# A pre-norm transformer block with routed experts on one core: block counts of the tensor-engine tiles read a turn ahead, gelus awaited singly, and the first batch's stacks moved through two DMA queues

## The chip, the core and the metric

The kernel runs on one core of one Trainium2 chip. Its engines are PE (TensorE, the matrix engine), ACT (ScalarE), DVE (VectorE), POOL (GpSimd) and SP (SyncE, which here only issues DMA transfers). The metric is the device time of one execution in microseconds (us); the kernel before has a median of 927.51 us over 3 runs (927.06 to 932.16).

## What is computed

The input x is 8 batches of 512 rows of 128 floats. Two blocks follow, each added to x:

```python
x = x + attn(layernorm(x))      # RMS norm; q, k, v; 16 heads of 8; then
#   lin: causal linear attention on Taylor features of q @ Wqf and k @ Wkf (order 2)
#   win: softmax attention, each query sees itself and 64 keys before it
#   attn(h) = h + concat(lin, win) @ Wout
x = x + ffn(layernorm(x))       # 8 experts, the two best of each row weighted
#   experts 0..3 (kind 0, "plain"): gelu(h @ W1 + b1) @ W2 + b2
#   experts 4..7 (kind 1, "kan"): basis functions of the layer norm of h, times kan_W0, a
#                                 second layer norm, basis functions again, times kan_W1
```

Which rows go to which expert depends on the data, so the number of tiles of each kind is known only on the chip.

## The kernel before, in words

All five engines have an instruction stream of their own, and semaphores order them. There are three stages.

**The prologue** (the streams up to `batches()`) prepares weights and the front of batch 0. DVE copies a mask pattern from PSUM (`band`, line 1027, once PE has raised `band_mm`), spreads it over two of three "stacks" of batch 0 (line 1030) and clears the PSUM tile `pv` (line 1036). PE transposes the normed rows (line 1425) and forms q, k and u (line 1428, SPLIT = q, k, u; u is the key side seen through the feature weights). Each is split into a half-precision part and a remainder: ACT writes `hi` (line 867), DVE writes `lo` (line 1042). SP stores `hi` and `lo` to the scratch `hl_d` in HBM (line 473: six stores of 128 KB, each pair awaiting its `lo`) and loads them back, rearranged by head, into the rows of the stacks (lines 448 and 450: 256 KB and 128 KB, one pair for each of the three stacks, semaphore `stack_loaded[0]`). SP then waits for all of them, and only then loads the rows `xb` of batch 1 (line 480). ACT clears a stack of batch 1 (line 875) after its part of the front; DVE spreads the pattern over the other two (line 1030 again).

**The batches.** `ORDER` lists the steps of a batch by hand; every engine walks the same list, `PROGRAM`, and does its part of each step. L, M and W are products on PE (lines 1588, 1569, 1601), each into one of three PSUM slots that ACT (lines 927, 936) or DVE (line 1185) frees; P is line 1629. Words with a plus are the front of the next batch: `stats` and `aggr` (DVE lines 994, 1003), `coef` (POOL lines 672 to 682 and the normed rows at line 691), `hT` (PE line 1425). POOL also masks diagonal blocks after an L step (line 766), and it scatters the routing records by indirect DMA (line 810). The step `out` is PE line 1688. The last batch is interleaved with the first tiles of the experts (`TAIL`, steps `ehid`, `efirst`, ...).

**The tiles.** A tile is 512 routed rows of one expert, four blocks of 128; a table in SBUF (`tab_i`, `tab_first`) gives for each tile its place, its expert and its number of filled blocks. A loop of UNROLL = 12 turns handles in turn k: for plain tiles `mlp_first(u+1)` in two parts (line 1475), `mlp_second(u+1)` (line 1493); for kan tiles `hidden_transposed(u)` (line 1530), `kan_first(u+1)` (line 1509), `rows_transposed` (line 1450) and `kan_second(u)` (line 1542). PE reads the number of blocks with `load_blocks`, a load from SBUF into a register of PE's sequencer, inside each of `mlp_first` (so twice a turn), `mlp_second`, `kan_first` and `kan_second`. In `mlp_first` it stands behind four waits:

```python
pe.wait_ge(m_y, tile_no(k, back=1))
if parts[-1] > 1:
    pe.wait_ge(m_g, tile_no(k, F // P, parts[-1] - 1))
...
with pe.If(load_blocks(0, k) > 2):
```

`m_g` counts the gelus of a tile (ACT line 885); the second part, `range(2, 4)`, writes the two PSUM banks that the first two gelus read. With more than two blocks both halves of 256 columns are multiplied, else one. DVE does the basis functions (line 1118), the statistics and the norm of the hidden rows (lines 1124 to 1141), and the weighting (lines 1103, 1107). POOL, in each turn, gathers kan rows (line 735), computes four norm coefficients (`hidden_coefficients`, line 760), scatter-adds the plain result (line 745), gathers plain rows, awaits that scatter, scatter-adds the kan result and awaits that (`end_of_add`).

## Time and profile before

| what | value |
|---|---|
| median of 3 runs | 927.51 us |
| the profiled execution | 928.66 us, of which its span in the trace is 926.8 us |
| PE, PE weight load | 765.3 us (83%), 571.6 us (62%) |
| ACT, POOL, DVE | 533.1 us (58%), 491.9 us (53%), 465.0 us (50%) |
| mean granted TensorE clock | 0.925 of full speed |

All moments below are microseconds from the start of the span: the prologue lasts to about 32, the batches to about 507, the tiles from there to the end. An engine's time is busy time; the time between is given with what ended it. "issue" is idle time for which the trace shows no semaphore: the sequencer was reading a register, branching or fetching.

### The profile page before, as it was taken

The page shows a single profiled execution, that of the slowest core. Times are in us where ns is not written, and L with a number is a line of the kernel's source. Part 1 is how long each engine was busy: PE and PEld are TensorE (multiplying, and loading weights), DVE is VectorE, ACT ScalarE, POOL GpSimd, SP SyncE. Part 2 cuts the span into 40 slices and gives each one's busy share as a digit, 9 for nine tenths or more (in the row PEclk, how much of TensorE's full clock was granted, in tenths as well). Part 3 has the DMA queues.
Part 4 walks back from the last instruction along what each step waited for, and adds up shares of the span by engine and source line. Part 5 has one row for each costly group of instructions (what it writes and reads, how often), then busy time and mean ns, then how long its engine had stood idle before and what let it go on. Part 6 is the DMA issues. An engine that isn't in the chain of part 4 may idle for free.

```text
span 926.8 us, 20634 instructions
## 1 busy us (share of the span) xinstructions
PE 765.3 (83%) x7113; PEld 571.6 (62%) x7114; DVE 465.0 (50%) x1076; ACT 533.1 (58%) x697; POOL 491.9 (53%) x699
## 2 busy tenths in 40 slices
PE   4599979799798797988945857999999999999870
PEld 2246555465454554546513645888988898889770
DVE  6525516355163362643501664565867785787330
ACT  4477756567475575666714626366677666766410
POOL 8334536545265254651572347548677767764431
PEclk9799989989899898999966979899999999999975
DMA  2330402204013040030162316255456446443213
GB/s 60 114 99 2 123 12 64 71 2 125 10 46 88 2 122 13 34 101 2 42 100 50 131 15 165 47 138 132 72 150 155 112 94 147 131 73 61 22 17 106
DMA packets 93698, 70.72 MB, mean 76 GB/s; under 512 B 41602, under 2 KB 85922, under 8 KB 91684
## 3 DMA queue, kind: packets, MB, share of 16 engines
q1 hardware_dynamic: 76660, 57.74, 22.0%
q0 software_dynamic: 16912, 11.35, 8.9%
q8 instruction: 72, 1.18, 0.6%
q14 instruction: 54, 0.44, 0.2%
HBM read 49.51 MB, written 21.36 MB: 76 GB/s over the span
## 4 chain that ended last, share of the span: by engine, by line
PE 59%; ACT 11%; DVE 9%; issue 9%; POOL 4%; another core or an unknown queue 4%; DMA 1%; SPq 0%; DVEq 0%; ACTq 0%; POOLq 0%
PE pv L1542 12%; PE ring L1509 12%; PE pv L1629 10%; ACT Pb L927 4%; PE ring L1601 4%; PE ring L1588 4%; PE ring L1475 3%; PE ring L1493 3%; ACT Pb L936 2%; DVE maxima L1185 2%; PE ring L1688 2%; DVE h L1237 2%; PE ring L1569 2%; PE ring L1428 1%
## 5 line engine op out<-in xcount | busy, mean ns | idle before, releaser
L927 ACT ACTIVATE Pb<-ring 128x1024 f32<-128x1024 f32 x160 | 156.5, 1025 | 64.6 <-PE ring L1588 62.8
L766 POOL TENSOR_SCALAR_AFFINE_SELECT Pb<-Pb 128x512 f32<-128x512 f32 x128 | 79.3, 637 | 208.7 <-ACT Pb L927 208.7
L745 POOL DMA_INDIRECT acc_d<-stack,srec x84 | 138.2, 1645 | 69.9 <-issue 35.8
L1629 PE MATMUL pv<-Pb,vaug 128*32 128x192 f32 (+4 forms) x2048 | 138.1, 399 | 18.3 <-issue 15.9
L936 ACT ACTIVATE Pb<-ring 128x768 f32<-128x768 f32 (+1 forms) x128 | 89.7, 759 | 98.1 <-remote 61.0
L1118 DVE SCALAR_TENSOR_TENSOR stack<-stack 128x512 f32<-128x512 f32 x160 | 103.3, 689 | 72.4 <-ACT stack L905 38.1
L1509 PE MATMUL ring<-stack 128*128 128x256 f32 x560 | 126.5, 383 | 8.4 <-issue 8.3
L1509 PEld LDWEIGHTS ring<-stack 128*128 128x128 f32 x560 | 106.0, 191 | 26.7 <-issue 12.4
L1629 PEld LDWEIGHTS pv<-Pb,vaug 128*32 128x32 f32 x2048 | 65.9, 117 | 82.0 <-issue 58.8
L905 ACT ACTIVATE stack<-ring,kprm 128x512 f32<-128x512 f32 x160 | 108.1, 814 | 0.1
L1588 PE MATMUL ring<-stack 128*128 128x128 f16 (+3 forms) x512 | 90.5, 306 | 18.0 <-issue 10.7
L1601 PE MATMUL ring<-stack 128*128 128x192 f16 (+1 forms) x512 | 63.3, 266 | 36.3 <-issue 22.5
L1185 DVE TENSOR_REDUCE maxima<-ring 128x8 f32<-128x1024 f32 x64 | 77.4, 1221 | 17.4 <-PE ring L1569 16.7
L1588 PEld LDWEIGHTS ring<-stack 128*128 128x128 f16 x512 | 42.1, 99 | 66.0 <-issue 17.4
L1601 PEld LDWEIGHTS ring<-stack 128*128 128x128 f16 x512 | 42.5, 107 | 56.3 <-issue 37.1
L810 POOL DMA_INDIRECT slot_d<-rec,pos x64 | 62.2, 973 | 25.6 <-issue 18.1
L1542 PE MATMUL pv<-stack 128*128 128x128 f32 x560 | 72.2, 281 | 1.1 <-DVE stack L1118 1.1
L885 ACT ACTIVATE Pb<-ring,mprm 128x512 f32<-128x512 f32 x44 | 27.9, 684 | 77.8 <-PE ring L1475 73.4
L1542 PEld LDWEIGHTS pv<-stack 128*128 128x128 f32 x560 | 67.8, 196 | 2.4 <-DVE stack L1118 2.2
L1196 DVE COPY y_sb<-pv 128x512 f32<-128x512 f32 x16 | 11.1, 692 | 115.9 <-PE pv L1629 96.8
L905 ACT ACTIVATE stack<-pv,kprm 128x512 f32<-128x512 f32 x80 | 55.2, 784 | 13.2 <-DVE stack L1118 10.7
L735 POOL DMA_INDIRECT stack<-n_d,grec x40 | 39.5, 988 | 34.1 <-issue 27.6
(232 smaller groups left out, 1171.3 us busy)
## 6 DMA issues: line engine op xcount, KB each, us to landing
stack<-L_ffn_kan_sl_W SPq DMA_DIRECT2D x20, 1024.0 KB
stack<-hl_d SPq DMA_DIRECT2D x24, 256.0 KB
stack<-hl_d SPq DMA_DIRECT2D x24, 128.0 KB
stack<-L_ffn_mlp_W SPq DMA_DIRECT2D x12, 256.0 KB
hl_d<-hi SPq DMA_DIRECT2D x7, 384.0 KB, 2.6
hl_d<-lo SPq DMA_DIRECT2D x7, 384.0 KB, 3.3
Pb<-L_ffn_mlp_W SPq DMA_DIRECT2D x10, 256.0 KB
xb<-L_attn_x SPq DMA_DIRECT2D x9, 256.0 KB
```

What stands on the lines that cost most here:

```text
L745: pool.indirect_dma_start(acc_d, bass.IndirectOffsetOnAxis(ap=srec[:, kind, u % RECS, q, 0:1], axis=0), src[:, u % 2, q, :], None, compute ...
L766: pool.affine_select(pd, pd, [[0, HG], [1, P]], ALU.is_ge, 0.0, base=0, channel_multiplier=-1).then_inc(pd_ready, 1)
L905: act.activation(sig[z][:, g % SIGS, :], src, ACT.Sigmoid, bias=bias, scale=scale).then_inc(k_sig[z], 1)
L927: act.activation(Pb[:, n % 2, at:at + 1024].rearrange("p (k q) -> p k q", k=2), slot(job), ACT.Square, bias=1.0).then_inc(freed[job % SLOT ...
L936: act.activation(Pb[:, n % 2, 768 * c:768 * (c + 1)].rearrange("p (k j q) -> p k j q", k=2, j=2)[:, :, :, 0:wq], slot(job)[:, :, 0:384].re ...
L1118: dve.scalar_tensor_tensor(basis[z][g], s_, -1.0, s_, ALU.add, ALU.mult).then_inc(k_bas[z], 1)
L1185: dve.tensor_reduce(maxima[:, c, 2 * HG * n:2 * HG * (n + 1)].rearrange("p (k j) -> p k j", j=HG), slot(job).rearrange("p k (j q) -> p k j ...
L1509: mm = pe.matmul(ring[:, 0, q // 2, F2 * (q % 2):F2 * (q % 2 + 1)], basis[0][g][:, P * q:P * (q + 1)], kw[u % 2][:, F2 * g:F2 * (g + 1)], ...
L1542: mm = pe.matmul(pv[:, 1, P * q:P * (q + 1)], basis[1][g][:, P * q:P * (q + 1)], kw[u % 2][:, 2048 + D * g:2048 + D * (g + 1)], start=(g = ...
L1588: mm = pe.matmul(slot(job)[:, bk, o:o + w], sk[:, head(n, hd), P * c:P * (c + 1)], su[:, head(n, hd), P * c:T], start=True, stop=True)
L1601: mm = pe.matmul(slot(job)[:, bk, WQ * jj:WQ * jj + wq], sk[:, h, P * c:P * (c + 1)], sq[:, h, P * c:P * c + wq], start=True, stop=True)
L1629: mm = pe.matmul(pv[32 * j:32 * (j + 1), n // 2 % 2, P * c:P * c + w], vaug[:, p, c, head(n, j) // 2, 16 * (n % 2):16 * (n % 2) + 32], src ...
```

## The change

1. In the tile loop PE reads the number of blocks of a plain tile once, before the preceding `kan_second`, and hands it to both parts of `mlp_first` and to `mlp_second`; for the first tile of the loop it is read at the top of the loop, and in the last batch before the first `ehid` step.
2. In `mlp_first` the wait on the gelus moves into the products: that of part f > 1 awaits gelu f - 2 alone.
3. In the prologue ACT stores `hi` from its own queue after each split, awaits the last store and loads stack 2 (256 KB and 128 KB); SP stores `lo` alone and loads stacks 0 and 1. SP loads `xb` of batch 1 before it awaits the stacks.
4. In the prologue DVE copies `band` before `m_blk`, and clears `pv` behind the three `lo`.

```diff
@@ sync (SP)
             for s in range(3):
                 sp.wait_ge(lo_ready, s + 1)
-                for part, half in enumerate((hi, lo)):
-                    sp.dma_start(hl_d[s, part], half[:, s, :]).then_inc(first_stored[s], 16)
-            for s in range(3):
+                sp.dma_start(hl_d[s, 1], lo[:, s, :]).then_inc(first_stored[s], 16)
+            for s in range(2):
                 sp.wait_ge(first_stored[s], 32)
-                load_stack(0, s)
+                load_stack(sp, 0, s)
+            sp.wait_ge(first_stored[2], 32)
             sp.sem_inc(hl_stored, 32)
-            sp.wait_ge(stack_loaded[0], STACK_DMAS)
             sp.wait_ge(xres_ready, 1)
             sp.dma_start(xb[:], x_rows[1]).then_inc(x_loaded, 16)
+            sp.wait_ge(stack_loaded[0], STACK_DMAS)
             sp.wait_ge(pads_ready, 2)
@@ scalar (ACT)
             for s in FRONT:
                 front(s, 0, 0, FRONT.index(s))
+                if s in SPLIT:
+                    m = SPLIT.index(s)
+                    act.wait_ge(hi_ready, m + 1)
+                    act.dma_start(hl_d[m, 0], hi[:, m, :]).then_inc(first_stored[m], 16)
+            act.wait_ge(stack0_zeroed, 3)
+            act.wait_ge(first_stored[2], 32)
+            load_stack(act, 0, 2)
             act.activation(stack[1][2][:].bitcast(F32), zeros, ACT.Copy).then_inc(stack1_zeroed, 1)
@@ vector (DVE)
+            dve.wait_ge(band_mm, 1)
+            link(dve.tensor_copy(band[:], pv[:]))
             dve.wait_ge(prep_mm, 1)
             dve.wait_ge(rows_ready, 1)
             dve.tensor_tensor(by_dim(m_blk[:]), by_head(slot(0)[:, 1, 0:P]), by_head(block[:]), ALU.mult).then_inc(prep_dve, 1)
...
-            dve.wait_ge(band_mm, 1)
-            link(dve.tensor_copy(band[:], pv[:]))
...
-            dve.memset(pv[:], 0.0).then_inc(pv_zeroed, 1)
...
             for s in FRONT:
                 if s in SPLIT:
                     front(s, 0, 0, FRONT.index(s))
+            dve.memset(pv[:], 0.0).then_inc(pv_zeroed, 1)
@@ tensor (PE)
-            def mlp_first(i, u, parts=range(F // P)):
+            def mlp_first(i, u, blocks, parts=range(F // P)):
...
-                if parts[-1] > 1:
-                    pe.wait_ge(m_g, tile_no(k, F // P, parts[-1] - 1))
                 half = TS // 2
 
                 def products(f, at):
+                    if f > 1:
+                        pe.wait_ge(m_g, tile_no(k, F // P, f - 1))
                     return pe.matmul(m_banks[(f + 1) % 2][:, at:at + half], mw[u % 2][:, P * f:P * (f + 1)],
                                      mxs[:, at:at + half], start=True, stop=True)
 
-                with pe.If(load_blocks(0, k) > 2):
+                with pe.If(blocks > 2):
...
-            def mlp_second(i, u):
+            def mlp_second(i, u, blocks):
                 k = i * UNROLL + u
-                blocks = load_blocks(0, k)
...
                     if s == "ehid":
-                        mlp_first(0, 0, [n])
+                        if n == 0:
+                            pe.wait_ge(first_ready, 1)
+                            m_blocks = load_blocks(0, 0)
+                        mlp_first(0, 0, m_blocks, [n])
...
                         k = i * UNROLL + u
+                        if u == 0:
+                            m_blocks = load_blocks(0, k + 1)
                         with pe.If(k + 1 < n_kind[0]):
-                            mlp_first(i, u + 1, range(0, 2))
+                            mlp_first(i, u + 1, m_blocks, range(0, 2))
...
                         with pe.If(k + 1 < n_kind[0]):
-                            mlp_second(i, u + 1)
+                            mlp_second(i, u + 1, m_blocks)
                         with pe.If(k + 2 < n_kind[1]):
                             rows_transposed(1, i, u + 2)
+                        if u + 1 < UNROLL:
+                            m_blocks = load_blocks(0, k + 2)
                         with pe.If(k < n_kind[1]):
                             kan_second(i, u)
```

`load_stack` and `stack_rows` are the functions of before, moved up, with the issuing engine as an argument.

## Rows read from the trace of the kernel before

**Rows 1.** The page, part 4: the chain that ended last, shares by engine.

```profile
PE 59%; ACT 11%; DVE 9%; issue 9%; POOL 4%; another core or an unknown queue 4%; DMA 1%; SPq 0%; DVEq 0%; ACTq 0%; POOLq 0%
```

**Rows 2.** Waits of PE, 553 to 880 us: line <- releaser: us in total, times, longest.

```profile
PE ring L1475 <- issue: 5.4, 7, 1.2
PE ring L1475 <- ACT Pb L885: 3.7, 4, 1.0
```

**Rows 3.** The chain in order of time, 505 to 675 us: start, us, what.

```profile
522.30 0.37 issue
...
551.73 0.93 issue
...
640.35 1.07 issue
```

**Rows 4.** Timeline of PE, 585 to 665 us: start, us, engine, line, operation.

```profile
657.19 1.95 PE L1493 MATMUL ring<-Pb 128*128 128x128 f32 x16
...
659.42 1.95 PE L1542 MATMUL pv<-stack 128*128 128x128 f32 x16
```

**Rows 5.** Timelines of POOL, PE and DVE in the tiles, 600 to 835 us.

```profile
607.48 1.61 POOL L745 DMA_INDIRECT acc_d<-stack,srec  x1 [3.06 <-DVE stack L1107]
...
661.31 0.19 POOL L760 TENSOR_TENSOR zc<-zmv,kconst 128x4 f32<-128x4 f32 x1 [1.07 <-DVE zmv L1134]
...
730.08 0.53 POOL L760 TENSOR_TENSOR zc<-zc,consts 128x4 f32<-128x4 f32 x1
...
732.34 1.09 PE L1530 MATMUL ring<-identf,Pb 128*128 128x128 f32 x8 [0.17 <-DVE Pb L1141]
...
826.62 0.52 POOL L760 TENSOR_TENSOR zc<-zc,consts 128x4 f32<-128x4 f32 x1
...
828.81 1.42 DVE L1141 TENSOR_SCALAR Pb<-Pb,zc 128x256 f32<-128x256 f32 x4
```

**Rows 6.** Timeline of all engines in the prologue, 0 to 50 us.

```profile
18.05 0.91 DVE L1036 MEMSET pv<- 128x1024 f32 x1 [0.21 <-issue]
...
20.89 0.69 DVE L1042 TENSOR_TENSOR lo<-ring,hi 128x512 f16<-128x512 f32 x1 [0.45 <-ACT hi L867]
...
21.58 3.61 ACT L875 ACTIVATE stack<-zero 128x4096 f32<-128x4096 f32 x1
...
21.98 0.44 SPq L473 DMA_DIRECT2D hl_d<-lo  x1
...
22.46 0.51 SPq L448 DMA_DIRECT2D stack<-hl_d  x1
...
25.58 0.64 SPq L450 DMA_DIRECT2D stack<-hl_d  x1
```

**Rows 7.** Timeline of the start of batch 0, 28 to 50 us.

```profile
31.73 2.72 PE L1588 MATMUL ring<-stack 128*128 128x256 f16 x10 [10.68 <-issue]
...
33.98 0.63 POOL L766 TENSOR_SCALAR_AFFINE_SELECT Pb<-Pb 128x512 f32<-128x512 f32 x1 [10.44 <-ACT Pb L927]
...
34.68 0.87 DVE L994 BATCH_NORM_STATS2 stats<-xb 128x6 f32<-128x128 f32 x4 [5.99 <-DMA xb<-L_attn_x]
...
36.05 0.20 POOL L672 TENSOR_TENSOR c<-mv,consts 128x4 f32<-128x4 f32 x1 [1.44 <-DVE mv L1003]
...
41.66 0.66 PE L1425 MATMUL ring<-identf,hn 128*128 128x128 f32 x4 [1.96 <-POOL hn L691]
```

**Rows 8.** The stores to `hl_d`, 15 to 36 us: issue to landing.

```profile
DMA to landing us min/median/max: 1.7/1.8/1.8
```

**Rows 9.** Busy time by stretch: stretch, length, PE, PEld, DVE, ACT, POOL, PEclk, DMA share, GB/s.

```profile
28.00:30.00 2.00, 0.00 (x0) 0.00 (x0) 0.69 (x1) 0.00 (x0) 0.00 (x0) 0.50 0.46 123
```

**Rows 10.** The chain in order of time: the step `out` of three successive batches.

```profile
144.34 2.02 PE ring L1688 x16
202.00 2.02 PE ring L1688 x16
262.35 2.02 PE ring L1688 x16
```

More of the change, by code:

```diff
@@ L399, in use_no, with stack_rows, load_stack @@
             return i * (UNROLL // buffers * per) + (u // buffers + 1) * per
+        def stack_rows(first, n):
+            return slice(SPREAD * first, SPREAD * (first + n - 1) + 1, SPREAD)
+        def load_stack(eng, u, s):
+            both = 0 if s != 1 else DH
+            hi_again = 2 * DH if s != 1 else 0
+            eng.dma_start(stack[u][s][stack_rows(both, 2 * DH), :], hl_d[s].rearrange("a (d h) t -> (a d) (h t)", d=DH)
+                         ).then_inc(stack_loaded[u], 16)
+            eng.dma_start(stack[u][s][stack_rows(hi_again, DH), :], hl_d[s, 0].rearrange("(d h) t -> d (h t)", d=DH)
+                         ).then_inc(stack_loaded[u], 16)
         W_DMAS = 6
@@ L438, in _ @@
             load_ones(0)
-            def stack_rows(first, n):
-                return slice(SPREAD * first, SPREAD * (first + n - 1) + 1, SPREAD)
-            def load_stack(u, s):
-                both = 0 if s != 1 else DH
-                hi_again = 2 * DH if s != 1 else 0
-                sp.dma_start(stack[u][s][stack_rows(both, 2 * DH), :], hl_d[s].rearrange("a (d h) t -> (a d) (h t)", d=DH)
-                             ).then_inc(stack_loaded[u], 16)
-                sp.dma_start(stack[u][s][stack_rows(hi_again, DH), :], hl_d[s, 0].rearrange("(d h) t -> d (h t)", d=DH)
-                             ).then_inc(stack_loaded[u], 16)
             def clear_shift(u):
@@ L464, in load_stacks @@
                 for s in range(3):
-                    load_stack(u, s)
+                    load_stack(sp, u, s)
                 clear_shift(u)
@@ L1660, in batches @@
                     if s == "esecond":
-                        mlp_second(0, 0)
+                        mlp_second(0, 0, m_blocks)
                     if s == "ytr":
@@ L1737, in _ @@
                         with pe.If(k + 1 < n_kind[0]):
-                            mlp_first(i, u + 1, range(2, 4))
+                            mlp_first(i, u + 1, m_blocks, range(2, 4))
                         with pe.If(k + 1 < n_kind[1]):
```

## The prediction, written before the changed kernel was built

> **What bounds the kernel now.** I read the page's chain first: PE holds 59% of it and "issue" 9% [rows 1]. So most of the time is PE working, and what can be had is where the chain leaves PE. The change touches two such places, so I read the waits of PE over the tiles, then the timelines around each.
>
> In the tiles PE stands idle before line 1475 eleven times in the loop: seven times for "issue", 5.4 us together, four times "for ACT", 3.7 us together [rows 2]. The chain shows what one is: the second gelu ends, 1.07 us pass with no event at all, and the products of f = 2 and 3 start [rows 3]. Nothing is computed in it. It is the register load with its branch, which stands behind the wait on the gelus, so PE's sequencer can begin it only when its queue has run dry. The four "for ACT" (3.7 / 4 = 0.93 us each) are the same thing: the gelu had ended long before. Two more lie ahead of the loop: 0.93 us after the first weighting, 0.37 us in the last batch [rows 3]. They lie on the chain, since PE works without a break after them.
>
> In the prologue PE waits 10.68 us for the stacks [rows 7]. SP issues their six loads from 22.46 to 26.22 [rows 6], and the first product starts at 31.73. Then a second wait follows: `xb` is issued when the stacks have landed, so DVE's statistics start at 34.68 after 5.99 us of waiting, POOL's coefficients at 36.05, and PE stands 1.96 us before the transposes of 41.66 [rows 7].
>
> **The change, part by part: the counts.** Removed on the chain: 5.4 + 3.7 + 0.93 + 0.37 = 10.4 us. Of each I leave 0.1 us for the branch and the semaphore, 1.2 us in all, so 9.2 us. The load that replaces them stands before `kan_second`, where another load already stood. Its cover is what PE still has queued. In a turn with two blocks 2.23 us lie between the start of line 1493 and that of line 1542, with the transposes of line 1450 between them and no gap for the one load there [rows 4]. One load with its branch costs 0.93 us when bare, two cost 1.86 us, less than that stretch. Cost: nothing, if PE's queue holds this much; if it holds only what one load needs, 0.93 us a turn (the rival below). The rows prove a cover of 0.93 us and no more. The Trainium skill, "TensorE: Matmul & The Clock Gate", section "Architectural detail: the array is 16× 32×32, not 1× 128×128", gives PE a queue of 64 instructions; 1.86 us of these products is some 34, so by the Trainium skill both loads are covered and the rival falls. No run here has shown the depth yet.
>
> Awaiting the gelus one by one gives next to nothing by itself. The transposes of line 1530 stand between the two parts, 1.09 us of them [rows 5], and so the two gelus are over about when the transposes are: the time without any event in rows 3 begins when both are. Bounds: 0 to 0.1 us a turn; I take 0.
>
> **What is late next.** POOL. Its turn is one chain of indirect DMAs and waits for their completion. It last waits for others at 607.48 (for DVE) and at 661.31, only 1.07 us for the statistics; from there it never waits for PE or DVE up to the coefficients that end at 730.61, on which DVE's norm and then PE's transposes at 732.34 follow at once [rows 5]. A faster PE doesn't move that chain. The 9.1 us of rows 2 are 0.9 us a turn over ten turns, 0.8 us after the 0.1 that stays. By 607.48, one turn in, PE has gained 0.37 + 0.93 + 0.9 - 0.3 = 1.9 us, and POOL can use 1.07 more at 661.31: it runs 3.0 us earlier. PE would by 732.34, after five turns, be 5.1 us earlier; it gets 3.0. Three turns on, at 828.81, it would have 2.4 more; there DVE's norm followed its own work, and POOL's coefficients had ended at 827.14 [rows 5], so 1.6 of it counts. The last two turns give 1.6. **Sum of the counts: 3.0 + 1.6 + 1.6 = 6.2 us**, between 6.2 (POOL as rigid as this) and 9.2 (POOL's waits shrink with the rest).
>
> **The prologue.** The band copy fills DVE's idle time, but the next step waits for the normed rows, so it brings some 0.15 us. The clearing of `pv` (0.91 us [rows 6]) moves out of the way of the first `lo`; the last `lo`, 20.89 to 21.58, waits for its `hi`, which waits for PE, and stays. Behind it now stand the pads, POOL's store of them and the spreading over the stacks of batch 1, all 0.9 us later: DVE ends at 29.6 instead of 28.69 [rows 9], before PE starts. ACT issues three stores, 0.44 us each as on SP [rows 6], while it waits for PE anyhow. Then it stands until the last `lo` has landed: SP issues that at 21.6, behind no `hi` now, and a store takes 1.8 us [rows 8], so 23.4. It issues two loads to 24.7 and only then clears the stack: 3.61 us [rows 6], to 28.4, before PE's first product, which is the next thing ACT waits for. SP's four loads run from 22.05 to 24.5.
>
> How much earlier do the stacks land? The last issue ends at 24.7 instead of 26.2: at most 1.5 us. But the same bytes move, and `xb`, 256 KB, now moves among them; at the 123 GB/s of 28 to 30 us and a share of 0.46 [rows 9], a full share moves 267 GB/s, so `xb` alone takes 1.0 us: at worst the stacks land 1.0 us later. The share of 0.46 itself leaves room for `xb`, so I take the upper half: 0.7 us earlier. The Trainium skill, "Trainium Kernel Development and Optimization", section "Key Constraints", speaks against the two queues: DMAs issued from SP and ACT share the same engines, and only the issue time is saved. By it the gain is the issue time or less, which is my upper bound; that the landing lags the last issue by 5.4 us here agrees with it.
>
> With `xb` early, the statistics start when DVE is free, at 29.6, and are aggregated by 30.9. POOL's coefficients then follow its mask, which ends at 34.61 - 0.7 = 33.9, so they start at 33.95 instead of 36.05: **2.1 us earlier**. The normed rows are done at 39.5, PE arrives at 41.66 - 1.96 - 0.7 = 39.0: it waits for them, and goes 2.1 us earlier. Ends: 1.44 + 1.5 = 2.9 us, and 1.44 - 1.0 = 0.4 us (1.44 is POOL's wait in rows 7). From there the batches are the same list of steps, shifted.
>
> **Sum.** 6.2 + 2.1 = 8.3 us. The profiled execution took 928.66 us, so 920.4 us; the median of the runs is 1.15 us below it: **919.2 us**.
>
> **The rivals.**
> (a) POOL gives way: its waits for scatters are DMA time that may shift with the weight loads that PE triggers. Then all 9.2 us count: 927.5 - 11.3 = 916.2 us.
> (b) The prologue brings nothing, as the loads are bound by the transfers and `xb` delays them: 0.4 us instead of 2.1: 927.5 - 6.6 = 920.9 us.
> (c) The second load before `kan_second` is bare. The change then only moves the stall: ten turns of 0.93 us come back, and the counts bring about nothing; with the prologue 925.4 us. Against it: the load is hidden there today without trace. In the worst case that part of the change does not do what it says.
> (d) Slower: while POOL scatters the records (line 810), the other engines stutter in some batches and not in others. From one `out` to the next it is 57.66 us, then 60.35 us [rows 10], 2.7 us more for the same steps. ACT's and SP's streams now have other lengths and other phases to the DMA traffic. If the five undisturbed batches fell into it, 13.5 us would be added: 927.5 - 8.3 + 13.5 = 932.7 us. The sign turns with the fourth batch. Against it: from batch 1 on everything shifts together.
>
> **How the numbers follow.** Forecast 0.40; (a) 0.22; (b) 0.14; (c) 0.11; (d) 0.06; 0.07 for stutters that shrink instead, some 912 us. A measurement tells 0.5%, 4.6 us, from no change. Below 922.9 us lie the forecast, (a), (b) and the last, less 0.04 for their upper ends: 0.79. Within 0.5%: (c), these ends, and less than it would need of (d): 0.15. Slower: (d) in full, 0.06. The range from 913.5 to 925.5 holds the forecast with its bounds, (a), (b) and half of (c).
>
> **What would show it.** In the profile of the changed kernel: PE idle before line 1475's counterpart below 2 us in all, with 1 us where before it was 10; no new "issue" before line 1542's (else (c)); PE waiting for DVE's norm at one transposition or two, 2 to 3 us there, with POOL's coefficients ending just before (else (a)); the first product near 31.0, statistics near 29.9, transposes of the next front near 39.6 (else (b)); spacings of `out` of 57.5 us where they were so (else (d)). I am wrong if PE's gaps go and the end doesn't move, or if the stacks land later than 31.7.

## The result, and the profile after

The changed kernel took 918.09 us (median of 20 runs, 914.3 to 924.85) against 929.32 us before (20 runs beside it, 919.52 to 934.01): ratio 0.9889, interval 0.987 to 0.9909. The profiled execution took 916.61 us, its span is 914.8 us. 919.2 us was predicted. The time lies within 1.1 us of that, but part of this is luck: the kernel before took 929.32 us beside it and not 927.51 us, so the gain is 11.2 us where 8.3 us were predicted. Three terms behind the total don't fit either, and the experiments are about these.

The page's chain, part 4, answers to [rows 1]:

```profile
PE 63%; ACT 10%; DVE 8%; issue 7%; another core or an unknown queue 5%; POOL 4%; DMA 2%; DVEq 0%; ACTq 0%; POOLq 0%
```

PE's share rose from 59% to 63%, that of "issue" fell from 9% to 7%. The waits of PE from 553 to 880 us, which answer to [rows 2] (line 1475 is now 1482, 1493 is 1499, 1509 is 1515, 1542 is 1548; line <- releaser: us in total, times, longest):

```profile
PE ring L1499 <- issue: 7.7, 7, 1.8
PE ring L1515 <- issue: 2.6, 6, 0.6
PE pv L1548 <- issue: 1.8, 4, 0.5
PE pv L1548 <- DVE stack L1125: 1.1, 5, 0.3
PE ring L1499 <- ACT Pb L892: 0.6, 1, 0.6
```

Line 1482 is not in the list: all of the 9.1 us of [rows 2] are gone. But two waits for "issue" stand before the two kan layers, 2.6 us before the first and 1.8 us before the second. The forecast had none of them; in the trace before, the loop has 0.8 us before the first and nothing before the second. (The 7.7 us at line 1499 are one stutter ahead of the loop, from 570 to 580 us, where PE starts one product at a time; the trace before has it from 572 to 584.)

The timelines of POOL, DVE and PE in the tiles, where [rows 5] had coefficients, norm and transposes closely in a row:

```profile
703.17 1.61 POOL L745 DMA_INDIRECT acc_d<-stack,srec  x1 [0.30 <-issue]
...
713.52 1.01 POOL L735 DMA_INDIRECT stack<-n_d,grec  x1 [2.77 <-issue]
...
720.57 0.53 POOL L760 TENSOR_TENSOR zc<-zc,consts 128x4 f32<-128x4 f32 x1
...
725.04 1.09 PE L1536 MATMUL ring<-identf,Pb 128*128 128x128 f32 x8
...
819.84 1.53 DVE L1148 TENSOR_SCALAR Pb<-Pb,zc 128x256 f32<-128x256 f32 x4
```

PE's transposes at 725.04 wait for nobody, and stand 7.3 us earlier than before. POOL's coefficients end at 721.10, 9.5 us earlier than the 730.61 of [rows 5]. 4.4 us of both had been gained before the loop began (its first product moved from 589.5 to 585.1), so within the loop PE gained 2.9 us by then and POOL 5.1. So POOL did not stay where it was. The scatter at 703.17 shows one place where it gave way: it follows 0.30 us behind the gather, where in the trace before it had waited for its own DMAs:

```profile
712.54 1.61 POOL L745 DMA_INDIRECT acc_d<-stack,srec  x1 [3.04 <-issue]
```

The start of batch 0, as in [rows 7], and the stretch of [rows 9]:

```profile
25.00 0.39 SPq L479 DMA_DIRECT2D xb<-L_attn_x  x1
...
31.59 2.72 PE L1594 MATMUL ring<-stack 128*128 128x256 f16 x10 [10.05 <-DMA stack<-hl_d]
32.23 0.87 DVE L1001 BATCH_NORM_STATS2 stats<-xb 128x6 f32<-128x128 f32 x4 [2.13 <-DMA xb<-L_attn_x]
...
34.44 0.20 POOL L672 TENSOR_TENSOR c<-mv,consts 128x4 f32<-128x4 f32 x1
...
40.08 0.66 PE L1432 MATMUL ring<-identf,hn 128*128 128x128 f32 x4 [1.29 <-POOL hn L691]
```

```profile
28.00:30.00 2.00, 0.00 (x0) 0.00 (x0) 2.00 (x1) 1.38 (x1) 0.00 (x0) 0.50 0.78 281
```

The first product is only 0.14 us earlier, the statistics 2.45 us, the transposes of the next front 1.58 us. `xb` is issued at 25.00, lands at 32.2, and DVE waits for it, although it was free at 30.1. In the two microseconds in which the prediction saw room for it, with 123 GB/s moved [rows 9], 281 GB/s are moved now.

Where the 12.0 us between the two spans arose, from the starts of the same steps: 1.58 us up to the transposes of the next front; 1.0 more by the eighth `out` (512.98, now 510.40); 1.8 more by the first product of the second kan layer (589.5, now 585.1); 6.9 in the loop up to its last (896.7, now 885.4); 0.7 behind it. How much of each is chance, one pair of profiles can't say. Of one piece it can: towards the end of the loop the granted clock is at its lower level, 0.50 of full speed (1.2 GHz), in every profile of this document. Before, that stretch lasts some 10 us (880 to 890), after, some 7 us (870.5 to 877.5), as in the other profiles. PE's waits in the loop fell by 5.2 us (11.5 to 6.3), its busy time by 1.9 (295.8 to 293.8). The shorter stretch at half speed, some 3.4 us less, makes an estimated 1.7 us of the latter, and the edit did not aim at it.

### The profile page after: what moved, and what is told of

The parts are those of the page before. It is cut to its first block, busy times and chain, and to the rows that moved or that the text cites. A ratio compares the mean times of both kernels' runs of the same rounds, so it can differ in the third digit from the quotient of the medians.

```text
span 914.8 us, 20572 instructions
## 1 busy us (share of the span) xinstructions
PE 762.3 (83%) x7113; PEld 571.3 (62%) x7114; DVE 465.9 (51%) x1076; ACT 533.6 (58%) x697; POOL 493.0 (54%) x699
## 4 chain that ended last, share of the span: by engine, by line
PE 63%; ACT 10%; DVE 8%; issue 7%; another core or an unknown queue 5%; POOL 4%; DMA 2%; DVEq 0%; ACTq 0%; POOLq 0%
PE pv L1548 14%; PE ring L1515 12%; PE pv L1635 10%; PE ring L1607 4%; ACT Pb L934 4%; PE ring L1594 4%; PE ring L1482 3%; PE ring L1499 3%; ACT Pb L943 2%; DVE maxima L1192 2%; PE ring L1697 2%; PE ring L1575 2%; PE ring L1435 2%; DVE h L1244 1%
## 5 line engine op out<-in xcount | busy, mean ns | idle before, releaser
L1515 PE MATMUL ring<-stack 128*128 128x256 f32 x560 | 124.0, 381 | 2.6 <-issue 2.6
L1203 DVE COPY y_sb<-pv 128x512 f32<-128x512 f32 x16 | 11.1, 692 | 116.8 <-PE pv L1635 105.5
L1548 PEld LDWEIGHTS pv<-stack 128*128 128x128 f32 x560 | 66.5, 194 | 6.0 <-issue 3.5
```

What stands on the lines that cost most here:

```text
L1515: mm = pe.matmul(ring[:, 0, q // 2, F2 * (q % 2):F2 * (q % 2 + 1)], basis[0][g][:, P * q:P * (q + 1)], kw[u % 2][:, F2 * g:F2 * (g + 1)], ...
L1548: mm = pe.matmul(pv[:, 1, P * q:P * (q + 1)], basis[1][g][:, P * q:P * (q + 1)], kw[u % 2][:, 2048 + D * g:2048 + D * (g + 1)], start=(g = ...
```

## The experiments

They ran in three groups, each on a chip of its own, and by their times none was the chip of the first pair: the kernel before takes 866 us there instead of 929, in every group; more of that at the end. One profile of each kernel was taken. The quantity that repeats best is the **loop**: the time from the first to the last product of the second kan layer, read from the row of that line. The last column has PE's waits for "issue" before the products of f = 2 and 3 (those "for ACT" included) and before the two kan layers, and the waits for DVE's norm:

```
kernel           first to last      loop, us   waits of PE in the loop that matter
before           589.5 to 896.7     307.2      f = 2, 3: 8.3;  kan first 0.8
before_again     524.4 to 830.7     306.3      f = 2, 3: 8.2;  kan first 1.0, second 0.2
prologue_only    530.7 to 837.2     306.5      (tiles as before)
xb_only          522.7 to 828.9     306.2      (tiles as before)
two_queues       533.3 to 839.3     306.0      (tiles as before)
after            585.1 to 885.4     300.3      kan first 2.6, second 1.8
after_again      523.9 to 825.5     301.6      kan first 2.6, second 1.8
tiles_only       526.8 to 828.1     301.3      kan first 2.5, second 1.9
gelus_only       529.1 to 829.0     299.9      f = 2, 3: 1.4;  kan first 2.3, second 0.5
counts_only      529.6 to 831.9     302.3      f = 2, 3: 1.8;  kan first 0.7, second 1.7
load_moved       521.5 to 820.0     298.5      kan first 2.6, second 0
shared           529.2 to 831.6     302.4      kan first 0, second 0;  norm 7.6
third_load       531.4 to 837.4     306.0      kan first 2.7, second 5.9
pool_slower      530.0 to 838.6     308.6      kan first 2.5, second 1.9;  norm 5.1
```

Five profiles with the old tiles lie between 306.0 and 307.2 (mean 306.4), three with the new between 300.3 and 301.6 (mean 301.1). So the loop gained 5.4 us, and differences of a microsecond or less can't be told here. (Of the 9.1 us of [rows 2], 0.8 is a gap at 557.80, ahead of the loop; 8.3 are left in it.)

### Unchanged, once more: before_again and after_again

> The kernel before, unchanged, for its profile on the same chip as the other three of this group. Theory: the tile loop, from the first product of the second kan layer to its last, takes about 307 us as in rows of the trace before (589.5 to 896.7), whatever the batches take. The other four kernels' batches ran some 50 us shorter than in the trace of before; if that belongs to the chip, the last `out` here comes near 463 us again, and the 8.5 + 5.5 us of 'issue' before the products of the batches are gone in this kernel too; if it belongs to the edits, it comes near 513.

> The changed kernel, unchanged. Theory: gain in the tile loop 6 to 7 us, in the stretch from the last `out` to the loop some 1.5 us, in the prologue 1.6 us, 9 to 10 us in all, ratio 0.989 to 0.990. Rival, that the 12 us of the two first profiles held 2 to 3 us of chance in the batches and in the last granted clock: ratio 0.992. PE's 'issue' before the first kan products 2.6 us in 6, before the second 1.8 us in 4, as in the first trace of it.

Measured: 864.16 us for before_again, ratio 0.9989 [0.9954, 1.0024]; 857.9 us for after_again, ratio 0.9884 [0.9828, 0.9939]. The gain is the same on this chip, though 60 us of batches are missing. Waits of PE, 500 to 830 us, in before_again:

```profile
PE ring L1475 <- issue: 4.5, 5, 1.2
PE ring L1475 <- ACT Pb L885: 3.7, 4, 0.9
PE ring L1450 <- DMA vaug<-h_d,grec: 1.3, 1, 1.3
...
PE ring L1509 <- issue: 1.0, 3, 0.5
```

and from 490 to 830 us in after_again:

```profile
PE ring L1457 <- DMA vaug<-h_d,grec: 3.3, 1, 3.3
PE ring L1515 <- issue: 2.6, 6, 0.6
PE pv L1548 <- issue: 1.8, 4, 0.5
```

8.2 us went; 3.2 us came back before the kan layers (4.4 for 1.0 + 0.2). The net is 5.0 us, and the two loops differ by 4.7. So PE's waits account for the difference of the loops, and POOL held neither: PE waited for DVE's norm 0.8 us in the one and 0.2 us in the other. The expectation had 6 to 7 us for the loop, which came from the first pair; by the estimate above 1.7 us of that pair's 6.9 was the clock.

The two gaps ahead of the loop brought nothing. PE reaches the first kan products earlier, then waits for the gathered rows. In before_again the step reads

```profile
503.74 13.98 PE L1509 MATMUL ring<-stack 128*128 128x256 f32 x64
518.97 0.65 PE L1450 MATMUL ring<-identf,vaug 128*128 128x128 f32 x4 [1.26 <-DMA vaug<-h_d,grec]
```

and in after_again

```profile
500.21 14.02 PE L1515 MATMUL ring<-stack 128*128 128x256 f32 x64
517.52 0.65 PE L1457 MATMUL ring<-identf,vaug 128*128 128x128 f32 x4 [3.29 <-DMA vaug<-h_d,grec]
```

PE is 3.5 us earlier at the products and 1.45 us at the transposes, of which it had 1.3 us at the eighth `out` (457.59, 456.30); 2.0 us went into a longer wait for a DMA that POOL issues. Over the whole stretch from the eighth `out` to the loop the four kernels with old tiles took 66.5 to 66.8 us (before_again, prologue_only, xb_only, two_queues), those with new 67.6 and 66.9 (after_again, tiles_only). The 1.5 us that were expected here did not come. In the first pair the stretch held a stutter in each trace, so its 1.8 us say nothing.

### The parts of the change: tiles_only, prologue_only, gelus_only, counts_only

> The kernel before with the tile part of the change alone (counts read ahead, gelus awaited one by one); the prologue is that of before. Theory: in the two traces, PE's gaps before line 1475 went and the tiles ended about 9 us earlier after them, the prologue gave 1.55 us of the rest. So this kernel should take about 9.5 us less than the kernel before (ratio 0.990), with the first product at 31.7, the next front's transposes at 41.7 us as in before, and no 'issue' ahead of the f = 2 and 3 products. Rival, that the tiles' gain is capped by POOL at 6.2 us as in the sum: ratio 0.9935. Rival, that the gain is mostly drift of the batches between runs: ratio 0.997 or more.

> The kernel before with the prologue part alone (two queues, xb before the stacks' wait, DVE's order). Theory: it gives what the trace of the changed kernel shows at the next front's transposes, 1.6 us (40.08 for 41.66), of which only 0.14 us is the landing of the stacks; so 1.5 us of 927, ratio 0.998, hardly to be told from 1. In the profile: first product at 31.6, statistics on xb at 32.2, POOL's coefficients at 34.4. Rival (the sum's step): 2.1 us. Rival, that it is taken up again later by the batches' own waits: nothing, ratio 1.000.

> The kernel before with the waits on the gelus one by one, the counts still read inside the first-layer function. Theory (the sum's step): the load with its branch still stands ahead of the products, now ahead of the waits on the gelus. It then starts as soon as PE's sequencer gets there, while the transposes of line 1530 run, instead of behind the gelu: so most of the gap goes with this alone. If so PE's 'issue' and 'ACT' gaps before the f = 2 products shrink from 9.1 us to below 3 and the ratio is about 0.992. Rival: the individual waits give nothing, as the prediction took them at 0 to 0.1 us a turn, and the gaps stay near 9 us: ratio 1.000.

> The kernel before with the counts read a turn ahead, but the wait for both gelus kept as one ahead of the f = 2 and 3 products. Theory: the gap of about 0.9 us a turn goes as in the changed kernel, since without a load behind it a wait costs next to nothing; only the branch on the count stands behind it, some 0.1 us. Ratio within 0.001 of the tile part as a whole, some 0.990 to 0.991. Rival: branch and wait together still cost 0.3 us or more a turn, 'issue' before the f = 2 products stays at 3 us or more, ratio 0.993 or more.

`gelus_only` and `counts_only`, against the kernel before (excerpts):

```
 # gelus_only
-                if parts[-1] > 1:
-                    pe.wait_ge(m_g, tile_no(k, F // P, parts[-1] - 1))
...
                 def products(f, at):
+                    if f > 1:
+                        pe.wait_ge(m_g, tile_no(k, F // P, f - 1))
 # counts_only
-                with pe.If(load_blocks(0, k) > 2):
+                with pe.If(blocks > 2):
...
+                        if u + 1 < UNROLL:
+                            m_blocks = load_blocks(0, k + 2)
                         with pe.If(k < n_kind[1]):
                             kan_second(i, u)
```

Measured, as ratios to the kernel before: tiles_only 0.9934 [0.9894, 0.9975], prologue_only 0.9968 [0.9935, 1.0001], gelus_only 0.9936 [0.9902, 0.9971], counts_only 0.9982 [0.994, 1.0024]. The intervals are wider than most of what they should tell apart, so the profiles decide. tiles_only and prologue_only multiply to 0.990, about the change as a whole. tiles_only landed on the ratio of the rival in which POOL caps the gain (0.9935), but not by that mechanism: in its loop PE waits nowhere for the norm. In prologue_only the first product stands at 31.25, the statistics at 32.11 and the transposes of the next front at 39.73; 1.6 us were expected there, and of the time the interval lets nothing be said.

**gelus_only is the surprise.** Its loop took 299.9 us, as little as the whole tile part. Waits of PE, 500 to 830 us:

```profile
PE ring L1509 <- issue: 2.3, 6, 0.6
PE ring L1475 <- issue: 1.4, 3, 0.6
...
PE pv L1542 <- issue: 0.5, 1, 0.5
```

8.2 us before line 1475 fell to 1.4 with no load moved, as its expectation had it. The load had been expensive for its place behind the wait; ahead of it, it can run while the transposes of line 1530 do. The forecast priced this part at 0 to 0.1 us a turn. That holds only once the load is gone; alone, it takes most of the same gap. The two parts of the change are two cures for one stall.

counts_only took the gap too (waits of PE, 490 to 830 us):

```profile
PE ring L1475 <- ACT Pb L885: 1.8, 8, 0.3
PE pv L1541 <- issue: 1.7, 4, 0.5
...
PE ring L1508 <- issue: 0.7, 3, 0.3
```

A wait and a branch without a load cost 0.2 us each (1.8 us in eight), not the 0.9 of before. The loop of counts_only is 4.1 us shorter than the old mean, but its time missed the expectation: 0.990 to 0.991 lies outside the interval. Why the time shows less than the loop is open. Set against tiles_only, this kernel also shows where the 2.5 us before the first kan layer come from: with one wait for both gelus they are 0.7 us in three, with single waits 2.5 us in six. My reading: when the second gelu is awaited just before the last products, little is queued on PE as the load of the first kan layer begins. So what the single waits save before f = 2 (1.8 us) they pay one step later. In that narrow sense the forecast's zero was right.

### Depth of PE's queue: load_moved, third_load, shared

> The changed kernel with the read-ahead of the plain tile's count moved from just before the second kan layer (where another load stands) to just behind the products of the first kan layer. Theory: two loads in a row there exceed what PE still has queued, by 0.45 us in four turns; moved, each load stands alone behind some 2 us of queued products, and 'issue' before the second kan products goes from 1.8 us to 0.2 or less; the 2.6 us before the first kan products stay or fall. The time falls by 1 to 2 us, ratio to the changed kernel 0.998 to 0.999. Rival, that the 0.45 us come from the waits for the second layer's basis functions or for the weights, and not from the second load: 'issue' stays at 1.8 us and the time stays.

```
                         with pe.If(k + 1 < n_kind[1]):
                             kan_first(i, u + 1)
+                        if u + 1 < UNROLL:
+                            next_m = load_blocks(0, k + 2)
...
                         if u + 1 < UNROLL:
-                            m_blocks = load_blocks(0, k + 2)
+                            m_blocks = next_m
```

Measured: 856.41 us, ratio 0.9878 [0.9823, 0.9932]; after_again has 0.9884 beside it, so the times don't separate them. In the profile "issue" before the second kan products, 1.8 us before, is no longer among the waits, that before the first is unchanged:

```profile
PE ring L1515 <- issue: 2.6, 6, 0.5
PE ring L1536 <- DVE Pb L1148: 1.5, 2, 0.9
PE pv L1548 <- DVE stack L1125: 0.9, 5, 0.2
```

The second load in a row was the cause, as expected. The loop took 298.5 us, the shortest of all, 2.6 below the mean of the changed kernel. The waits explain little of that: 1.8 us of "issue" went, but PE now waits for DVE's norm, behind POOL, 1.5 us, and all its waits in the loop add up to 6.2 us for 6.7. The other 2 us are in its busy time (292.2 for 294.2), at the same granted clock of 0.99, and are not explained. The profile is of the fastest of this kernel's six runs.

> The changed kernel with one more read of the same count, into a register nobody uses, just before the second kan layer: three loads stand there in a row instead of two. Theory: with two, 'issue' before the second kan products was 1.8 us in 4 turns, 0.45 each, so the queued work covers about 1.4 us of the 1.86 in those turns; a third load has no cover left there and adds a full load, some 0.6 to 0.9 us a turn: 'issue' there rises to 7 to 10 us and the time by 4 to 8 us. Rival, that PE's queue still has much left where the second load was hidden (six of ten turns): 'issue' rises by less than 3 us.

```
                         if u + 1 < UNROLL:
                             m_blocks = load_blocks(0, k + 2)
+                            load_blocks(0, k + 2)
```

Measured: 865.7 us, ratio to the kernel before 0.9996 [0.9964, 1.0028]: the gain of the whole change is gone. Waits of PE, 490 to 850 us:

```profile
PE pv L1548 <- issue: 5.9, 7, 1.2
```

4.1 us more than with two loads, in three more turns, and the loop is 4.9 us above the mean of the changed kernel. (By the ratios some 10 us were lost. The edit does nothing ahead of the loop, yet the eighth `out` stands at 463.91 here and at 456.30 in after_again; the changed kernel was not run on this chip.) That is under half of what ten bare loads, those that nothing queued covers, would cost (9.3 us) and more than the rival allowed (under 3): between the two. In three turns of ten even the third is covered.

> load_moved, and the kan tile's count is read once a tile instead of twice, a turn ahead, just before the second kan layer; both kan layers of the next tile use it. Two loads a turn are left of three, each alone. Theory: the first kan layer's load was partly bare because its turn begins with the products of two hidden blocks only; without it 'issue' before the first kan products falls from 2.6 us to under 0.5. With the 1.8 us of the second layer, 4 us of PE's idle time go. If PE sets the pace, the time falls by 3 to 4 us against the changed kernel, ratio to the kernel before about 0.985. Rival, that POOL's chain of scatters and waits for them sets the pace in the loop: PE's idle time comes back as waits for DVE's norm behind POOL's coefficients, and the time falls by less than 1.5 us.

```
-                blocks = load_blocks(1, k)
...
+                            m_blocks = next_m
+                            far_k = load_blocks(1, k + 2)
                         with pe.If(k < n_kind[1]):
-                            kan_second(i, u)
+                            kan_second(i, u, k_blocks)
+                        if u + 1 < UNROLL:
+                            k_blocks, next_k = next_k, far_k
```

Measured: 859.55 us, ratio 0.9874 [0.9833, 0.9915]; loop 302.4 us, no shorter than with three loads. All "issue" is gone from the kan layers, and one wait stands in its place. Waits of PE, then its timeline:

```profile
PE ring L1535 <- DVE Pb L1148: 7.6, 2, 7.2
```

```profile
662.99 1.89 PE L1482 MATMUL ring<-Pb,stack 128*128 128x256 f32 x8
672.06 1.97 PE L1535 MATMUL ring<-identf,Pb 128*128 128x128 f32 x8 [7.18 <-DVE Pb L1148]
673.81 3.45 PE L1482 MATMUL ring<-Pb,stack 128*128 128x256 f32 x8
```

The DVE wait behind it, and what POOL did (timelines):

```profile
670.55 1.38 DVE L1148 TENSOR_SCALAR Pb<-Pb,zc 128x256 f32<-128x256 f32 x4 [6.61 <-POOL zc L760]
```

```profile
651.54 1.82 POOL L745 DMA_INDIRECT acc_d<-stack,srec  x1 [2.86 <-issue]
...
663.41 1.41 POOL L735 DMA_INDIRECT stack<-n_d,grec  x1 [4.45 <-issue]
```

POOL's coefficients stand behind gathers, and these behind the completion of scatters: 2.86 and 4.45 us of waiting in one turn. This is the cap that the prediction set at the fifth turn, in the same place. That PE arrives early is only part of it. In load_moved PE waits 0.93 us in this turn. Counted from the start of each loop, PE comes 2.6 us earlier here, but POOL's coefficients come 3.6 us later, since its two waits were 1.59 and 2.94 us there. What set the completion times of those DMAs was not tried, and this profile is of the slowest of the kernel's nine runs: the ratio 0.9874 is no worse than load_moved's 0.9878.

The wait costs more than its length. While PE stood idle, the granted clock fell to its lower level: it is 1.00 up to 670 us, 0.50 from 671 to 676, and 1.00 again from 677. Behind the wait the transposes took 1.97 us for 1.09 in load_moved, and eight products 3.45 us for 1.89 just before: 2.4 us more.

### POOL: pool_slower

> The changed kernel with one more power operation on POOL per tile, between the first and the second of the norm's coefficients, 1.04 to 1.38 us each, its result overwritten later: some 11 to 12 us of POOL's time over the loop. Theory: POOL's chain has little slack left in the changed kernel, since its waits for DVE and PE are 27 us in all but in three or four turns only, and elsewhere it waits for its own DMAs; the loop (301.6 us from the first to the last product of the second kan layer) grows by 3 to 8 us, as waits of PE for DVE's norm. Rival a, that POOL gives way through its waits for scatters and gathers: below 1.5 us. Rival b, that it sets the pace in every turn: 11 us.

```
                         (zmv[:, :, 0], zc[:, 1, :], ALU.mult), (zc[:, 2, :], minus, ALU.mult))):
+                    if c == 1:
+                        pool.tensor_tensor(zc[:, 3, :], a, b_, op)
                     pool.tensor_tensor(zc[:, c, :], a, b_, op).then_inc(k_cf, 1)
```

Measured: 867.05 us, ratio 0.9995 [0.9959, 1.0031]; loop 308.6 us, 7.5 above the changed kernel's mean.

```profile
674.99 1.91 PE L1538 MATMUL ring<-identf,Pb 128*128 128x128 f32 x8 [4.86 <-DVE Pb L1150]
```

In one turn of ten PE waits 4.86 us for the norm, in another 0.29; elsewhere the longer chain is hidden by what POOL waits for anyhow. The cap is real and sits in a single turn, the same as in `shared`. Of the other 2.4 us of the loop 1.7 stand right behind this wait: the granted clock is 0.52 from 675 to 678, the transposes take 1.91 us for 1.09 and the eight products after them 2.79 for 1.89. The rest has no row of its own here.

### The prologue: xb_only and two_queues

> The kernel before with one edit: xb is issued ahead of the wait for the stacks' landing, all on SP. Read from its profile. Five profiles with the prologue of before have the first product at 31.42 to 31.93 (mean 31.65) and the next front's transposes at 41.40 to 41.80 (mean 41.63); five with the new prologue at 30.81 to 31.80 (31.26) and 39.34 to 40.67 (39.90). Theory: the stacks' landing is bound by the transfers, so xb among them delays it a little (first product 31.7 to 32.3), the statistics run at 32.5 to 33 instead of 34.6, and nearly all of the gain comes from this edit: transposes at 40.2 to 40.6. Rival (the sum's bound): xb costs the stacks 1.0 us (first product 32.7) and the transposes come at 41.0 or later.

```
-            sp.wait_ge(stack_loaded[0], STACK_DMAS)
             sp.wait_ge(xres_ready, 1)
             sp.dma_start(xb[:], x_rows[1]).then_inc(x_loaded, 16)
+            sp.wait_ge(stack_loaded[0], STACK_DMAS)
```

> The kernel before with the stores of hi and the last stack's two loads moved to ACT, xb where it was, DVE's order that of before. Read from its profile. Theory: the last load is issued about 0.5 us earlier and the transfers bind, so the first product comes 0.3 to 0.7 us earlier, at 31.0 to 31.3, and the transposes by no more than that, at 41.0 to 41.3. Rival (the sum's upper bound): issue time binds, 1.5 us earlier, first product at 30.2. Rival: no gain at all, 31.5 or later.

Its edit is the change's own in `load_stack`, in SP's stores and loads and in ACT's three stores and two loads, with `xb` and DVE's order left as they were. Both took as long as the kernel before within their intervals (1.0005 and 1.0022). Their profiles, first xb_only:

```profile
31.97 2.72 PE L1588 MATMUL ring<-stack 128*128 128x256 f16 x10 [11.13 <-DMA stack<-hl_d]
32.68 0.87 DVE L994 BATCH_NORM_STATS2 stats<-xb 128x6 f32<-128x128 f32 x4 [4.20 <-DMA xb<-L_attn_x]
...
40.45 0.66 PE L1425 MATMUL ring<-identf,hn 128*128 128x128 f32 x4 [0.88 <-POOL hn L691]
```

then two_queues:

```profile
23.80 1.52 ACTq L411 DMA_DIRECT2D stack<-hl_d  x1
30.06 0.39 SPq L480 DMA_DIRECT2D xb<-L_attn_x  x1
30.14 2.72 PE L1595 MATMUL ring<-stack 128*128 128x256 f16 x10 [9.31 <-DMA stack<-hl_d]
...
40.18 1.11 PE L1432 MATMUL ring<-identf,hn 128*128 128x128 f32 x4 [1.98 <-POOL hn L691]
```

```
                        first product        next front's transposes
before (5 profiles)     31.65                41.63
xb early alone          31.97   +0.3         40.45   -1.2
two queues alone        30.14   -1.5         40.18   -1.45
both (7 profiles)       31.39   -0.3         39.99   -1.6
```

(The seven are the five that the expectation names, third_load and pool_slower.) My theory at this point, that the transfers bind the stacks, fell. Without `xb` among them, the stacks land 1.5 us earlier on two queues, which was the upper bound of the prediction. With it the first product is 1.25 us later again. 0.3 us of that is not `xb`: the last load of the stacks is issued at 24.11 in the mean of the seven and at 23.80 in two_queues, since the third `hi` came later (20.31 for 19.94). From that issue to the first product it takes 7.3 us (6.8 to 7.6) for 6.3, so some 0.9 us are left for `xb`. DVE's order differs between the two as well and was not tried alone. Each part alone brings most of the gain at the transposes, and together they bring little more. One profile each stands behind xb_only and two_queues; those of one kind spread by 0.5 us (old) and 1.0 us (new) at the first product.

## Why the prediction was right, and where it was not

**What bounds.** Right: the gap before f = 2 and 3 was the load behind the wait. With the load ahead of the wait, or taken out from behind it, most of the gap went (8.2 us to 1.4 in gelus_only, to 1.8 in counts_only). Under 2 us were predicted before that line in the changed kernel; in the loop there is none.

**The residue of 0.1 us** for wait and branch: in the changed kernel no gap is left to hold it; with the wait kept whole it is 0.2.

**"Cost: nothing" for the second load** was wrong in size. It cost 1.8 us in four turns of ten, which load_moved took away. Rival (c) had 9: the truth is a fifth of it. The cover read from [rows 4] was taken from one turn, whose 2.23 us begin with products that had been queued in time; in four turns, as I read it, they had not. The rule of the Trainium skill, "TensorE: Matmul & The Clock Gate", section "Architectural detail: the array is 16× 32×32, not 1× 128×128", is about how many instructions the queue can hold. It doesn't say how many are in it when the load begins, and the prediction used it as if it did. The prediction concluded from it that both loads are covered and the rival falls; 1.8 us here, and 5.9 us with a third load, say otherwise.

**Left out altogether:** the load of the first kan layer, which I never touched in the sum. It lost its cover, 1.6 us (2.6 for 1.0), as the gelus were awaited singly.

**POOL as next limit** was right as a place and wrong as a term here. I charged 3 us to it in the loop; neither profile of the changed kernel waits there more than 0.2 us. The prediction's reading that POOL waits for nobody between 661 and 730 us is right, though the trace names PE at two waits there (3.34 us before 687.61, 2.81 us before 722.92): the gather needs PE's transposes of the turn before, and in the changed kernel it starts at 713.52, ahead of those of its own turn (714.90). At least one of its waits for a scatter shrank (3.04 us to 0.30), as rival (a) had it; what sets their length was not tested. shared and pool_slower make the cap bind, in the turn that the prediction named. The loop's term was 5.1 us (6.2 less 1.1 ahead of it), or 4.4 with the gap at 557.80 put ahead of the loop, where it stands; it measured 5.4. That they lie so close is luck: the two errors, 3.2 us of new bare loads that I did not charge and some 3 us of POOL that I did, cancel.

**The 1.1 us ahead of the loop:** nothing. The gathered rows became the wait, 3.29 us for 1.26.

**The prologue:** 2.1 us foreseen, 1.58 measured in the first pair, 1.6 in the mean of seven. The step that failed is "the statistics start when DVE is free": they start at 32.2, when `xb` lands, not at 29.6. In the stacks' landing I took 0.7 us and got 0.3; the last issue ended at 25.7, not at 24.7. Both bounds came out nearly as worked out, 1.5 us by two_queues and 1.0 us for `xb` (some 0.9). The Trainium skill, "Trainium Kernel Development and Optimization", section "Key Constraints", says that issuing DMAs from several engines only saves the sequencer's issue time. The trace agrees in size: in two_queues the issue of the last load begins 1.8 us and ends 0.9 us earlier than in the kernels before (23.80 to 25.32 for 25.62 to 26.27), and the first product is 1.5 us earlier.

**Rival (d)**, the slower one, didn't come: from one `out` to the next the changed kernel takes 57.9 us (84.92 to 142.79), then 58.0 (to 200.75), where [rows 10] and the ones around them have 57.7 to 60.4. A later one takes 61.4 us (258.74 to 320.14), for 60.9 before: the stutter is still there in one batch.

**The sum.** Prologue 1.6 and loop 5.4 make 7.0 us of 929, 0.992. The ratios of the whole, 0.9889 and 0.9884, are 3 to 4 us better. The first interval (0.987 to 0.9909) does not hold 0.992, and barely misses the forecast's own ratio, 0.9910; it does hold rival (a)'s, 0.9878, whose 9.2 us from the tiles did not come either. So some of the gain lies where my readings don't reach; the eighth `out` scatters by 9 us between profiles with the same batches (454.7 in load_moved, 464.1 in prologue_only, both with the new prologue), which hides it. That stays open.

## What to carry to other kernels

A register load behind a semaphore wait was paid in full here, 0.9 us each, since the wait had drained the queue: read the count ahead of the wait, or a turn early behind a long run of queued products, and one load to a place. Before calling a load hidden, look at every turn for what is queued when it starts, and at the next load down the stream as well. A transfer that is pulled forward beside a critical one can take back what a second queue has won, here some 0.9 of 1.5 us. And when PE is made to wait, look at the granted clock behind the wait as well: 7.2 us of waiting cost another 2.4.

## What the runs showed of the hardware that was not expected

The same kernel takes 929 us in the first pair's runs and 866 on the three chips of the experiments. The loop is the same (307.2 and 306.3 us); the batches are not: from the first `out` to the eighth it is 426.5 us (86.50 to 512.98) in the first profile and 369.7 us (87.89 to 457.59) in before_again. The waits from 85 to 440 us of the kernel before, in its first profile, hold these rows ("remote" is another core or an unknown queue; the program has one core):

```profile
ACT Pb L936 <- remote: 42.8, 18, 5.8
...
DVE y_sb L1196 <- remote: 19.1, 2, 11.1
```

and in before_again both are smaller, the second a single wait of 5.0 us:

```profile
ACT Pb L936 <- remote: 11.9, 4, 3.3
```

Pieces of up to 11.1 us, in which the engines wait for something that the profile can't name, come more often in the first. PE's clock goes with them: from the first to the eighth `out` the granted clock is 0.92 of full speed in the first profile and 0.97 in before_again, and PE is busy 351.1 and 325.0 us with the same 4111 products. So 26 of the 57 us are PE at work, at the lower clock, and the rest is idle. Whether the waits pull the clock down or something else makes both was not tested. For readings of a few microseconds it means that stages without them are compared, not whole spans.
